# A softmax stage whose value matmuls run one slot's worth in every slot, in place of a fixed pattern

## The reference

```python
def _L1_attn_ref(x, pos_emb_k, Wq, Wk, Wv, Wproj):     # 16 heads of 8, B = 2, S = 1024
    q, k, v = (x @ Wq.T), (x @ Wk.T), (x @ Wv.T)        # each to (B, H, S, hd)
    att_rel_pos = jnp.einsum('bhsd,pd->bhsp', q, pos_emb_k)
    att_idxs = jnp.clip(ar[None, :] - ar[:, None], -r, r - 1) % P        # r = 128
    att_pos = att_rel_pos[:, :, ar[:, None], att_idxs]
    attn_val = jnp.einsum('bhqd,bhkd->bhqk', q, k)
    att = jax.nn.softmax((attn_val + att_pos) * attn_scale, axis=-1)
    y = jnp.einsum('bhqk,bhkd->bhqd', att, v)
    return y @ Wproj.T
```

## Time and profile before

| | us |
|---|---|
| median of 3 runs | 1114.95 |
| range of the runs | 1109.16 to 1116.31 |
| profiled execution, its time | 1107.29 |
| profiled execution, its span | 1105.4 |
| PE busy, of the span | 1020.1 (92%) |
| DVE busy | 756.4 (68%) |
| ACT busy | 729.0 (66%) |
| POOL busy | 541.9 (49%) |

### The profile page before, as it was taken

How to read it: one execution, slowest core, us unless ns; L and a number is a source line. 1 busy time by engine, 2 the same in 40 slices (tenths; PEclk the granted TensorE clock), 3 DMA queues, 4 the chain that set the end, 5 groups by cost and what they waited for, 6 DMA issues and landing times. The chain is left out here.

```text
span 1105.4 us, 22311 instructions
## 1 busy us (share of the span) xinstructions
PE 1020.1 (92%) x7828; PEld 639.4 (58%) x7828; DVE 756.4 (68%) x1707; ACT 729.0 (66%) x1090; POOL 541.9 (49%) x708
## 2 busy tenths in 40 slices
PE   3899999999998779999999999999999999999998
PEld 2444444678785545545454545554454567888886
DVE  7346241678866587787788788787877258686866
ACT  1699988556545337777777777777775666555553
POOL 1376776576544221344444544444222188565654
PEclk9999999999999858999999999999999999999999
DMA  4541231535465577999988988888773386343433
GB/s 164 192 133 59 88 105 45 150 124 171 138 198 169 191 210 223 261 281 261 254 257 258 255 240 231 235 241 241 237 225 107 91 250 149 122 123 124 122 124 98
DMA packets 146431, 197.41 MB, mean 179 GB/s; under 512 B 33293, under 2 KB 113150, under 8 KB 146286
## 3 DMA queue, kind: packets, MB, share of 16 engines
q1 hardware_dynamic: 126238, 184.32, 54.6%
q0 software_dynamic: 20064, 11.66, 6.2%
q10 hardware_dynamic: 16, 0.00, 0.0%
HBM read 123.00 MB, written 72.74 MB: 177 GB/s over the span
## 5 line engine op out<-in xcount | busy, mean ns | idle before, releaser
L1182 DVE TENSOR_REDUCE a_part<-a_duo 128x2 f32<-128x1024 f32 (+3 forms) x256 | 215.5, 855 | 13.3 <-PE a_duo L998 11.7
L765 POOL DMA_DIRECT2D scr_y1c<-ys x240 | 118.9, 504 | 188.9 <-DVE ys L1151 186.2
L1175 DVE CUSTOM_DVE_ANT_0 a_band_sum<-a_duo,a_rel_raw 128x256 f32<-128x256 f32 (+2 forms) x320 | 131.3, 447 | 79.5 <-PE a_duo L998 60.1
L1611 POOL TENSOR_TENSOR f_hid_lo<-f_hid,att 128x512 fp32r<-128x512 f32 (+1 forms) x100 | 130.0, 1301 | 90.2 <-ACT att L1576 88.6
L1011 PE MATMUL a_duo<-att 32*128 32x512 f32 (+3 forms) x672 | 138.1, 409 | 15.9 <-DVE a_part L1182 13.5
L1120 ACT ACTIVATE a_rel<-a_rel_ps 128x384 f32<-128x384 f32 x240 | 117.4, 489 | 48.2 <-PE a_rel_ps L985 43.1
L716 ACT ACTIVATE a_probs<-a_duo 128x1024 f32<-128x1024 f32 x192 | 139.8, 829 | 13.8 <-PE a_duo L665 12.4
L998 PE MATMUL a_duo<-att 31*128 31x512 f32 (+3 forms) x672 | 144.9, 427 | 0.7 <-DVE a_rows L1200 0.7
L1745 DVE TENSOR_TENSOR f_hid<-f_u,w_share 128x512 f32<-128x512 f32 (+1 forms) x168 | 116.2, 692 | 37.0 <-DMA w_share<-scr_cw 12.8
L1611 POOL TENSOR_TENSOR f_hid_lo<-f_hid,f_hid_hi 128x512 fp32r<-128x512 f32 x68 | 88.4, 1301 | 76.4 <-ACT f_hid_hi L1576 76.4
L654 POOL TENSOR_TENSOR a_probs<-a_probs,const 128x256 f32<-128x256 f32 x128 | 100.5, 804 | 49.1 <-ACT a_probs L716 48.9
(11 more groups left out here) (284 smaller groups left out, 2046.7 us busy)
## 6 DMA issues: line engine op xcount, KB each, us to landing
a_rel_raw<-scr_rel SPq DMA_DIRECT2D x128, 384.0 KB, 4.6
scr_rel<-a_rel SPq DMA_DIRECT2D x120, 384.0 KB, 3.7
w_share<-scr_cw SPq DMA_DIRECT2D x144, 128.0 KB, 3.2
w_share<-scr_cw SPq DMA_DIRECT2D x44, 256.0 KB, 3.2
scr_y1c<-ys POOLq DMA_DIRECT2D x240, 8.0 KB, 3.8
w_share<-scr_cw SPq DMA_DIRECT2D x20, 192.0 KB, 3.0
w_share<-scr_cw SPq DMA_DIRECT2D x16, 224.0 KB, 3.1
att<-scr_q SPq DMA_DIRECT2D x36, 96.0 KB
```

The source lines that it names most:

```text
L765: eng.dma_start(scr["y1c"][w, b, head, :, at:at + T // 4], sb["ys"][32 * (2 * hd + c) + HD * w:32 * (2 * hd + c) + HD * (w + 1), h % 2, :] ...
L1175: ins = dve.tensor_tensor_reduce(band_sum[:, m % 2, hd, 0:wide], both[:, hd, (a - 4 * x) * P:(b - 4 * x) * P], rel_raw[:, e % RING, hd, (a ...
L1182: ins = dve.tensor_reduce(part[:, h % 2, x, :, j % 4], both[:, :, lo * P:hi * P], AX.X, ALU.max, negate=True)
L1611: pool.tensor_tensor(hid_lo[0:m, n % 4, :], hid[0:m, n % 2, :], f32(hid_hi[0:m, n % 4, :]), ALU.subtract).then_inc(lo_ready, 1)
```

## The change

`VALUES` becomes sixteen ones. The sum is 16 as before, so that after slot k exactly k − 2 values of the pair have been run: slot n runs the values of slot n − 3. Nothing else is edited.

```diff
--- before.py
+++ after.py
@@ -779,7 +779,7 @@
     RING = 16
     KEPT = 6
     TURN, STEP = 23, weights.early * P
-    VALUES = (2, 1, 0, 2, 0, 2, 0, 1, 1, 2, 1, 0, 2, 0, 2, 0)
+    VALUES = (1,) * 16
     KEYS = ((5, 0, 1, 6, 2, 7, 3, 4), (4, 0, 3, 5, 1, 6, 2, 7))
     with ExitStack() as ctx:
```

## The result

The changed kernel takes 1208.6 us (median of 4 runs, 1196.7 to 1233.5) against 1112.1 us of the kernel before (4 runs, 1107.9 to 1116.3): a ratio of 1.079, with a 95% interval of 1.069 to 1.088. The forecast was 1155 us, range 1138 to 1172, slower: the direction is right, and the rise is about twice the forecast 43 us. The profiled execution takes 1196.69 us with a span of 1194.8, 89.4 us more than the span before.

The account below looks back on a forecast made before the run. PE, nearly always busy in the softmax stage, was taken as the bound; 41 us for late copies plus 2 for router weights gave +43, so 1150 or 1158 by base, taken as 1155 us, range 1138 to 1172.

Parts of the forecast that it names:

- What bounds the kernel: Softmax stage, its undisturbed middle: PE 93% busy at full clock, its largest engine wait being `turned` for VectorE's `part`.
- main term: Slots 2 and 10: late last value delays VectorE's copy, the pass and next `turned`; +1.1 and +2.2 us.
- price of a turn: Accumulator copy in slots 2 and 10, 29 times: +2.8 us per two, 41 us in all.
- small term of 2 us for the router's weights: Eight places from n = 179 where VectorE also copies router weights; four lose their cover, 4 × 0.4, +2 us.
- Rival 1: Softmax stage: idle VectorE absorbs the copy's wait, only 13.4 us of batches stay, 1128 us; chance 0.07.
- rival 2: Softmax stage: single values fill PE's 29.4 us of waits for `part`, faster, 1099 us; chance 0.03.
- more batches: Values in 16 slots per pair instead of 10: +0.84 us per pair, +13.4 us over 16 pairs.
- the walk: Slot by slot sum over a pair of heads at full clock: 32.2 us new against 29.4 old.
- Rival 3: After each of 29 late copies the clock falls for 3.4 us: up to 49 us on top, 1205; chance 0.05.

Follow-up runs that it names:

- undo run: Changed kernel with slots 1 and 9 running two values and slots 2 and 10 none; 1118.6 us, ratio 1.012 to the kernel before.
- last two runs: One matmul in each of ten slots before slot 0, added to a two-slot-lag pattern (1116.3 us, ratio 1.006) and to the kernel before (1119.4 us, 1.008).
- third experiment: Changed kernel with VectorE's accumulator copy moved behind the pass of its slot; 1118.1 us, ratio 1.006 to the kernel before.

## Why the prediction was right and wrong

*What bounds the kernel, and the main term: right.* The late value, the copy waiting for it with the pass and `turned` behind, and the price of a turn came out to within 0.15 us at each step. Pairs at full clock take 32.15 us (forecast 32.2), and the part of the loss that is there at full clock is 44.1 us (forecast 43), shown in the run with the extra matmuls. The small term of 2 us for the router's weights was an upper end: from slot 178 on two pairs take 0.56 us more than the others in that run and 0.25 more in the kernel before, an estimate of 1.2 us for four such pairs.

*Rival 1, absorbed, and rival 2, evenness: wrong, as forecast.* The copy's wait of 1.96 us reached `turned`, which waited 1.61 us, and the kernel is slower. What evenness and more batches are worth together shows in the undo run, which keeps single values in twelve slots and stands at 1.012: the walk gives 29.7 against 29.4 us for that pattern, 5 us; the ratio makes it 13 us, with an interval from 2 to 24.

*Rival 3, the clock: this is the step that failed.* Its place and its sign were right, its price (at most 49 us) is close to the 45.3 measured, and it was given a chance of 0.05 and left outside the range. The argument against it was an average: "PE would still be busy some 28.2 of 32.2 us". PE's mean busy share in the stage is indeed 89% after (419.7 of 470 us) against 93% before, which looks harmless. But the waits do not spread over the 32 us, they stand in one place, 1.61 us of PE's queue in slot 3 and again in slot 11, and one such wait per pair is enough for falls. The forecast had worked out that length itself ("more than 1 us in one place") and then argued from the mean. With the clock as open as the rows left it, both cases belonged in the range.

*Luck in the rival's price.* The sum 29 × 3.4 = 99 us at the lower level, at half a microsecond each, put on the 1150 of the profiled execution, gives 1199, and 1196.7 was measured. But it is made of parts that were off in opposite ways: 18 falls in place of 29, half of them longer (112 us from 435 us on, and 128 us more than with the extra matmuls in all), and a price of 0.35 in place of 0.5.

The Trainium skill's rule that activity releases a throttled clock (TensorE: Matmul & The Clock Gate, "What's actually happening") had the direction: more activity in the wait kept the clock at 2.4 GHz for the whole stage. The last two runs do not agree with it as simply: in 391 to 409 us PE was 95% busy by the profile and the clock stayed at 1.2 GHz.

*What stays open.* What exactly takes the clock down. Falls follow the long waits, but 11 of 29 such waits brought none, and the clock also falls in the pattern with the copy behind the pass, where PE's gaps are short, and never in the middle of the stage in the kernel before, whose waits add up to more. And why the low stretch at the stage's start ended at 421 us before, and at about 434 us both in the changed kernel and in the one with the copy moved: these runs were not made to tell a different order from another draw. That stretch, and not only the batches, may be in the 0.6% of the third experiment: of the 12.3 us that its profiled execution is over before, 4.9 lie in the first pair of heads.

## What to carry to other kernels

Before moving work later on one engine, look in the program of the engine that consumes it for what stands behind the waiting instruction: here one slot of delay cost at most 1% with the copy behind the pass, and 44 us with the copy ahead of it before the clock's part. And where PE would gain a wait of over a microsecond in one place, price the fall of the clock as a case of its own and keep it in the range; the mean busy share, 89% here, did not rule it out, and it doubled the loss. A pattern with two, one and no values per slot can look arbitrary and still encode which slot must come first for another engine; undoing only the four slots at the two turns showed it in one run.

## What the runs showed of the hardware

- In a stage that is 89% busy, a wait of about 1.6 us of PE's queue was followed by a fall of the granted clock to 1.2 GHz at 18 of 29 places; with two extra 128x256 float32 matmuls in each such wait it stayed at 2.4 GHz at all 29, and the kernel became 45 us faster with more work.
- Time at the lower level cost 0.35 us per microsecond in this kernel, not 0.5. That part of the stage waits for VectorE and ScalarE at either level is the likely reason; no run tested it.
- Extra matmuls that fill PE's waits while the clock is already low (busy 17.2 of 18 us) did not bring it back, and the kernels with them took 0.8 to 1% longer than without.
